# Conditioned attention block: row sums over slabs added in pairs by POOL, V on four query quarters, bursts of four slabs, scores in three single PSUM banks

## What is computed

```python
def _sln(h, w, ln_g, ln_b, Wg, bg, Wb, bb):           # layer norm, gain and bias from the condition w
    ln = (h - mean(h)) / sqrt(var(h) + 1e-5) * ln_g + ln_b
    return (w @ Wg.T + bg)[:, None, :] * ln + (w @ Wb.T + bb)[:, None, :]

B, N, D, heads, hd = 4, 1024, 512, 16, 32
h = _sln(x, cond, ...)
q, k, v = split(h @ Wqkv.T + bqkv)                     # each B, heads, N, hd
energy = einsum('bhqd,bhkd->bhqk', q, k)               # not scaled
att = softmax(energy, axis=-1) / D ** 0.5
out = einsum('bhqk,bhkd->bhqd', att, v)                # then B, N, D
h1 = out @ Wp.T + bp + x
return _sln(h1, cond, ...) + h1
```

## Time and profile before

| | |
|---|---|
| runs | 1584.9, 1585.34, 1586.55 us (median 1585.34) |
| the profiled execution | 1583.32 us, span 1581.7 us |
| TensorE matmul | 1468.6 us busy, 93% |
| VectorE | 945.9 us, 60% |
| ScalarE | 655.1 us, 41% |
| POOL | 426.7 us, 27% |
| granted TensorE clock, mean | 0.976 |
| DMA | 176 MB, mean 111 GB/s |

### The profile page before, as it was taken

One profiled execution on the slowest core, in us unless ns is written; L12 is line 12 of the kernel. 1 busy time (PEld: TensorE's weight loads), 2 busy tenths in 40 slices (PEclk: granted clock), 3 DMA queues, 4 the chain that ended last, 5 costly groups with the idle time before them and its releaser, 6 DMA issues.

```text
span 1581.7 us, 28876 instructions
## 1 busy us (share of the span) xinstructions
PE 1468.6 (93%) x8756; PEld 832.5 (53%) x8756; DVE 945.9 (60%) x1697; ACT 655.1 (41%) x794; POOL 426.7 (27%) x523
## 2 busy tenths in 40 slices
PE   6998999999999999999999999999999999999733
PEld 4886645555554656555555556555444444344332
DVE  5336666565656566665656666565666665666145
ACT  3221444444444444444444444344444444445300
POOL 2442201111111233131423323121313231323357
PEclk9999999999999999999999999999999999999966
DMA  6799563645434676656454575556334242423142
GB/s 215 178 173 186 135 77 97 92 111 70 109 86 85 162 108 154 72 149 91 118 126 94 160 97 160 56 141 95 95 82 111 67 121 54 123 58 92 52 113 87
DMA packets 211534, 175.98 MB, mean 111 GB/s; under 512 B 102644, under 2 KB 177396, under 8 KB 211480
## 3 DMA queue, kind: packets, MB, share of 16 engines
q1 hardware_dynamic: 209176, 167.96, 50.6%
q0 software_dynamic: 2304, 7.34, 1.2%
HBM read 115.13 MB, written 59.31 MB: 110 GB/s over the span
## 4 chain that ended last, share of the span: by engine, by line
PE 79%; DVE 7%; SPq 4%; issue 3%; DMA 3%; POOL 2%; ACT 1%; POOLq 1%; DVEq 0%; ACTq 0%
PE ps_o L673 19%; PE ps_a L638 16%; PE ps_st L653 11%; PE ps_w L545 9%; PE ps_o L670 9%; PE ps_w L602 8%; DVE half_max L993 5%; PE ps_st L602 3%; SPq L401 1%; PE ps_o L545 1%; PE ps_w L591 1%; DMA scale_t<-rcp_scratch 1%; PE ps_a L632 0%; POOL oT_s L1159 0%; SPq L356 0%
## 5 line engine op out<-in xcount | busy, mean ns | idle before, releaser
L993 DVE TENSOR_REDUCE half_max<-ps_a 128x1 f32<-128x512 f32 x1024 | 689.2, 689 | 484.0 <-PE ps_a L638 478.6
L809 ACT ACTIVATE p<-ps_st 128x1024 f32<-128x1024 f32 x512 | 521.9, 1025 | 499.4 <-PE ps_st L653 495.0
L670 PE MATMUL ps_o<-p,v_head 128*32 128x512 f32 x2048 | 490.2, 600 | 0.0
L673 PE MATMUL ps_o<-p,v_head 128*1 128x512 f32 x2048 | 483.5, 593 | 0.0
L638 PE MATMUL ps_a<-k_stack,q_stack 96*128 96x512 f32 x1024 | 429.4, 432 | 23.7 <-DVEq L1001 7.2
L653 PE MATMUL ps_st<-q_stack,k_stack 98*128 98x512 f32 x1024 | 328.7, 402 | 6.7 <-DMA q_stack<-max_rows 6.7
L638 PEld LDWEIGHTS ps_a<-k_stack,q_stack 96*128 96x128 f32 x1024 | 190.5, 188 | 256.1 <-DVE half_max L993 122.6
L653 PEld LDWEIGHTS ps_st<-q_stack,k_stack 98*128 98x128 f32 x1024 | 188.7, 191 | 40.8 <-issue 10.5
L602 PEld LDWEIGHTS ps_w<-hT_s,wqkv_s 128*128 128x128 f32 x1056 | 146.4, 188 | 47.4 <-issue 36.9
L602 PE MATMUL ps_w<-hT_s,wqkv_s 128*128 128x256 f32 x1056 | 158.0, 285 | 0.0
L673 PEld LDWEIGHTS ps_o<-p,v_head 128*1 128x1 f32 x2048 | 69.8, 82 | 154.8 <-issue 154.8
(11 more groups left out here) (86 smaller groups left out, 1017.9 us busy)
## 6 DMA issues: line engine op xcount, KB each, us to landing
qk_scratch<-qkT_s SPq DMA_DIRECT2D x108, 256.0 KB, 2.4
q_stack<-qk_scratch SPq DMA_DIRECT2D x192, 128.0 KB, 3.0
k_stack<-qk_scratch SPq DMA_DIRECT2D x192, 128.0 KB, 3.3
v_scratch<-v_parts SPq DMA_DIRECT2D x32, 264.0 KB, 10.7
v_head<-v_scratch SPq DMA_DIRECT2D x64, 132.0 KB, 2.2
...
att_scratch<-o_stage SPq DMA_DIRECT2D x128, 64.0 KB, 1.6
```

The lines of the kernel that those rows point to most:

```text
L670: pe.matmul(ps_o[HD * e:HD * e + HD, :], v_head[:, s, k, 0:HD], p32[:, k, e * 512:(e + 1) * 512], start=(k == 0), stop=(k == 7))
L673: mm = pe.matmul(ps_o[64 + HD * e:65 + HD * e, :], v_head[:, s, k, HD:VP], p32[:, k, e * 512:(e + 1) * 512], start=(k == 0), stop=(k == 7))
L809: nc.scalar.activation(p32[:, k, :], scores, ACT.Exp).then_inc(exp_done, 1)
L993: V.tensor_reduce(half_max[:, s % 2, item:item + 1], ps_a[:, parity, :], AX.X, ALU.max).then_inc(a_used, 1)
```

## The change

- **V on quarters** (`weighted`). The four matmuls of a slab are V of the four quarters of 256 queries, in the four groups of partitions of ps_o. v_head loses its 33rd column.
- **Sums over added pairs** (`pair_add`, `pair_sums`). When V of slabs 2j and 2j + 1 is done, POOL adds slab 2j onto 2j + 1 in place, 128x1024. TensorE multiplies the result by a column of sqrt(512), again four quarters at once, into a bank of its own, ps_s.
- **Bursts of four slabs**. At k = 4 the burst has the sums of pairs 2 and 3 of the head before and V of slabs 0 to 3; at k = 0 the sums of pairs 0 and 1 and V of slabs 4 to 7, both of the head before. POOL's additions stand at its steps k = 5, 6 (pairs 0, 1) and k = 1, 2 of the next head (pairs 2, 3). An even slot of p32 is free after the addition, an odd one after the sum.
- **Three single banks of scores**. ps_st has three banks, used by half-slabs in the order of `ST_BANK`; a half's matmul waits for the exponential of three halves before (at the end of a head, two). `exps` takes each half by itself.
- `take_sums` is split in `take_out` (k = 2) and `take_sums` (k = 6), 256 columns each; SP has four stores for V (k = 4) and four for the sums (k = 7).
- Step tables: statistics of the next tiles from steps 5 and 13 to 5 and 9, out projection from 23, 24, 27, 28 to 21, 22, 25, 26, reciprocals from 7 to 9 and their store from 8 to 10, residual loads from 10 to 1, the other loads of the outs from 10 to 12, POOL's steps as below.

```diff
-OUT_STAGE = {23: (0, 1), 24: (0, 2), 27: (1, 1), 28: (1, 2)}
+OUT_STAGE = {21: (0, 1), 22: (0, 2), 25: (1, 1), 26: (1, 2)}
-LN_STEP = {5: 0, 13: 1}
-OUT_STATS_STEP = {27: 0, 31: 1}
-NORM_SCALE_STEP = {7: 0, 15: 1}
-NORM_GAIN_STEP = {9: 0, 17: 1}
-RESIDUAL_STEP = {9: 0, 13: 1}
+LN_STEP = {5: 0, 9: 1}
+OUT_STATS_STEP = {25: 0, 29: 1}
+PAIR_ADD_STEP = {1: 2, 2: 3, 5: 0, 6: 1}
+RESIDUAL_STEP = {3: 0, 4: 1}
+NORM_SCALE_STEP = {7: 0, 11: 1}
+NORM_GAIN_STEP = {8: 0, 12: 1}
+OUT_NORM_STEP = {15: 0, 16: 1}
+OUT_LOW_STEP = {19: 0, 20: 1}
 OUT_SCALE_STEP = {27: 0, 31: 1}
-OUT_FINISH_STEP = {29: 0, 31: 1}
+OUT_FINISH_STEP = {28: 0, 31: 1}
-RECIP_STEP = 7
+RECIP_STEP = 9
-OUT_LOAD_STEP = 10
+RESIDUAL_LOAD_STEP = 1
+OUT_LOAD_STEP = 12
...
+        ST_BANK = [0, 1, 2] * 5 + [1]
+        ST_AFTER = [r - 3 for r in range(15)] + [13]
+        ST_AFTER[0:3] = [12 - 16, 15 - 16, 14 - 16]
...
+                need(pe, exp_done, 64 * g + 16 * s + ST_AFTER[2 * k + e] + 1)
+                pe.matmul(ps_st[:, ST_BANK[2 * k + e], :], k_stack[0:98, s, k * 128:(k + 1) * 128],
+                          q_stack[0:98, s, e * 512:(e + 1) * 512], start=True, stop=True).then_inc(st_ready, 1)
...
+                if k % 2 == 0:
+                    pe.wait_ge(exp_done, 64 * g + 16 * s + 2 * k + 4)
+                for e in range(4):
+                    mm = pe.matmul(ps_o[HD * e:HD * e + HD, 0:QW], v_head[:, s, k, :], p32[:, k, e * QW:(e + 1) * QW],
                                    start=(k == 0), stop=(k == 7))
...
+            def pair_sums(g, s, j):
...
+                pe.wait_ge(pair_added, 16 * g + 4 * s + j + 1)
+                for e in range(4):
+                    mm = pe.matmul(ps_s[HD * e:HD * e + 1, 0:QW], root_s[:], p32[:, 2 * j + 1, e * QW:(e + 1) * QW],
+                                   start=(j == 0), stop=(j == 3))
+                mm.then_inc(sum_done, 1)
...
+                for e in range(2):
+                    act.wait_ge(st_ready, n + e + 1)
+                    if e == 0:
+                        need(act, sum_done if k % 2 else pair_added, freed)
+                    nc.scalar.activation(p32[:, k, e * 512:(e + 1) * 512], ps_st[:, ST_BANK[2 * k + e], :], ACT.Exp
+                                         ).then_inc(exp_done, 1)
...
+            def pair_add(g, s, j):
+                pool.wait_ge(pv_done, 16 * g + 4 * s + j + 1)
+                G.tensor_tensor(p32[:, 2 * j + 1, :], p32[:, 2 * j, :], p32[:, 2 * j + 1, :], ALU.add).then_inc(pair_added, 1)
```

More of the change, by code:

```diff
@@ L479, in iteration @@
                             store_row(u + 1, (s + 1) % 4)
+                        if k == 7 and not (first and s == 0):
+                            store_sums(u - 1, (s + 3) % 4)
+                        if outs and step == RESIDUAL_LOAD_STEP:
+                            for a in range(2):
+                                load_residual(pair, a)
                         if step == RECIP_STORE_STEP and not first:
@@ L719, in iteration @@
                             a_item(*use)
[L720 to L723 removed]
+                        after = (i, s, k + 1) if k < 7 else (i + (s + 1) // 4, (s + 1) % 4, 0)
+                        if last and (s, k) == (3, 7):
+                            after = None
+                        if after:
+                            turned_scores(*after, 0)
                         piece(step - 1, 1)
@@ L726, in iteration @@
                             a_item(*use)
-                        if k % 2:
-                            for j in (k - 3, k - 2):
-                                if j >= 0:
-                                    sums(i, s, j)
-                                elif not (first and s == 0):
-                                    sums(i - (s == 0), (s - 1) % 4, j + 8)
+                        if after:
+                            turned_scores(*after, 1)
+                        before = (i - (s == 0), (s - 1) % 4)
+                        if k == 0 and not (first and s == 0):
+                            for j in (0, 1):
+                                pair_sums(*before, j)
+                            for j in range(4, 8):
+                                weighted(*before, j)
+                        if k == 4:
+                            if not (first and s == 0):
+                                for j in (2, 3):
+                                    pair_sums(*before, j)
+                            for j in range(4):
+                                weighted(i, s, j)
                         piece(step, 0)
@@ L743, in _ @@
             iteration(ITERS - 1, False, True, last=True)
-            for k in (6, 7):
-                sums(ITERS - 1, 3, k)
+            for k in range(4, 8):
+                weighted(ITERS - 1, 3, k)
+            for j in range(4):
+                pair_sums(ITERS - 1, 3, j)
             for m in range(END, ITERS):
@@ L831, in iteration @@
                     if k == 2 and not (first and s == 0):
+                        take_out(4 * i + s - 1, (s + 3) % 4)
+                    if k == 6 and not (first and s == 0):
                         take_sums(4 * i + s - 1, (s + 3) % 4)
@@ L1213, in _, with iteration @@
                 norm(LEAD, a)
-            def iteration(i, tiles, norms, outs):
+            def iteration(i, tiles, norms, outs, first=False):
                 pair = i - FIRST_OUTS
@@ L1218, in iteration @@
                 for step in range(32):
+                    s, k = step // 8, step % 8
+                    if k in PAIR_ADD_STEP:
+                        j = PAIR_ADD_STEP[k]
+                        if j < 2:
+                            pair_add(i, s, j)
+                        elif not (first and s == 0):
+                            pair_add(i - (s == 0), (s - 1) % 4, j)
                     if norms and step in NORM_SCALE_STEP:
@@ L1244, in _ @@
             iteration(ITERS - 1, False, False, True)
+            for j in (2, 3):
+                pair_add(ITERS - 1, 3, j)
             residual(END, 0)
```

109 lines of the change are left out of this document (53 added, 56 removed).

## The result

The changed kernel takes 1672.2 us (median of four runs, 1660.8 to 1680.2) against 1585.9 for the kernel before beside it: ratio 1.054, 95% interval 1.046 to 1.061, so 5.4% slower. I had forecast 1605 with a range of 1543 to 1650. "Slower" held; the size didn't, and the time lies outside the range.

The account below looks back on a forecast made before the run. TensorE, busy 93% of the span, was taken to bound the kernel. 1583.3 + 12 (tiles and outs) - 6 (tiles alone) + 0 (outs alone) + 14 (end) = 1603, plus 2 to the median: 1605 us, range 1543 to 1650.

Parts of the forecast that it names:

- TensorE's saving: V and sum bursts: 2.4 us less a head, 152 us in all if nothing but TensorE counted.
- rival 2: TensorE's bursts: issue limits the quarter sets, 100 us above the forecast at the upper end, 1705; chance 0.07.
- rival 4: TensorE's bursts: sets run one after another instead of four at once, showing as a slower V; others 0.01.
- The walk through the stretches: Eight stretches between bursts of a pass, timed singly: +1.7 us with tiles and outs, -1.6 tiles alone, -0.1 outs alone.
- A: First stretch of a pass, steps 1 to 4: 7.15 us, 5.3 in outs-only passes.
- H: Last stretch of a pass, steps 29 to 32: 6.7 us, 5.9 with tiles alone.
- The out projection's wait for VectorE: Step 21, passes with tiles and outs: waits 1.9 us for VectorE's eviction; stretch 10.4 us instead of 8.3.
- The end: Last pass, step 21's transpose to taking the sums: 38 us instead of 25.1; +14 taken with two more stores.
- POOL's delay: Additions queued around out tiles delay step 36's burst: 2.3 us with tiles and outs, 4.2 with outs alone.
- two waits of a pass at L704: TensorE waiting on POOL's additions (L1259), the wait of step 4 of the next pass taking 2 to 4 us.
- rival 3: POOL's additions hold VectorE's cast and subtraction, up to 2.4 us each; 36 us over some 30 heads, 1640; chance 0.12.
- the row of maxima: Step 14, SP's late loads stand ahead of its DMA: 1 us of TensorE's wait kept in each outs-only pass.

Follow-up runs that it names:

- the loads split: Changed kernel with the small reductions, plus tile 1's att and scale loads moved from step 12 to step 14, behind the row of maxima: 1602.9 us, ratio 1.0063.
- the small reductions: Changed kernel with VectorE's cast and subtraction of the maxima written as small reductions over 128x16: 1633.3 us, ratio 1.031.
- the planted stall: Kernel before, with TensorE waiting at step 22 of each pass for a chain of six small POOL additions: 1657.6 us, ratio 1.039.

## Why the prediction was wrong, point by point

- **TensorE's saving** was right: a burst takes 2.70 us (12 x 0.2145 + 0.12), so sets are 0.2145 apart; rival 2 is out, and so is rival 4.
- **The walk through the stretches** was right. Where neither hold nor row disturbs, with the loads split, against the walk: passes with tiles, A 6.0 us (7.15), B 9.5 (9.7), C 10.0 (10.0), D 7.6 (8.0), E 8.8 (8.9), F 10.5 (10.4), G 7.1 (7.2), H 7.0 (6.7). Outs alone: 5.6, 5.2 and 5.1 for B, C and E (5.9, 5.6, 5.3), F 7.3 (7.6). A was 1.1 us too long, which is most of why tiles alone gained 2.5 us and not 1.6. The out projection's wait for VectorE came as told (11.7 us over seven passes).
- **The end**: 37.0 us for 38.
- **POOL's delay** came behind out tile 1 as told, and about in size, but at another wait: with step 36's burst I had only its own wait, and the exps of slab 4 wait for the same addition first (up to 4.1 us), with the turned scores behind them. The sign that I had named, two waits of a pass at L704, one of 2 to 4 us, didn't come: inside the loop none is over 0.6 us. Nor did L660 wait tens of us more than before (16.4 for 6.2).
- **The step that failed first is the hold of the casts, which the sum of 1603 put at nothing.** As rival 3, with 0.12, I named the place, steps 4 of heads with late additions, and the mechanism, and gave a hold at most one addition, 2.4 us, and 36 us at 1.2 in some 30 heads. The runs show 39 us by the small reductions, from eleven holds of 4.8 to 9.5 us, one a pass. That 36 is near 39 is luck: the number of holds and the size of each were both far off. The mistake was to take one POOL operation as the bound from the longest of L1011, when in the kernel before POOL seldom has two operations back to back there, and after the change up to six. And it was no rival: the sequence that I had worked out for POOL around the outs makes the row by itself, so it belonged in the sum.
- **The second is the row of maxima.** I kept 1 us of its wait in outs-only passes and none elsewhere, because the loads moved by two steps had "room". The earlier trace rows showed the same queue late already: row issued 3.8 us after its transpose. Moving eleven issues of 0.4 to 0.5 us two steps nearer cost 24 us of waits and 28 to 30 us of time.
- **The third is the clock.** No term had it. The waits that I did forecast were priced at their length; the planted stall shows 3.1 us costing 6.2. The half-clock time grew from 3 to 192 us, which is up to 94 us of lost time (half of 189), part of it beside waits. It isn't a term wholly beside the first two: with their gaps gone, 103 of the 192 us are left.
- With the first two taken away the kernel runs at 1602.9 us, where I had forecast 1605. That it fits so closely is partly luck: the kernel before took 1591.4 beside it, so it is 10 to 12 us slower where I had forecast 20; tiles alone gained 1 us a pass more than told, the last pass lost 4 more, and 103 us at half clock were in no term.
